# Decay attention: scores computed once and copied by ScalarE, the exponentials and the decay sharing one pair of PSUM banks

## The chip, the cores and the metric

One core of one Trainium2 chip runs a small language-model tower as one program. The metric is the device time in microseconds (us) of one execution; lower is better. A NeuronCore has TensorE (PE, matrix products, writes PSUM), VectorE (DVE), ScalarE (ACT, activation functions), GpSimd (POOL, which here works on SBUF alone) and DMA queues. Each engine takes its instructions in the order written, and engines wait for each other on semaphores.

## The reference, cut to what matters

The change lies in the attention of the second layer. For 128 sequences of 128 tokens, with 8 heads of width 8 and a causal mask, it computes

```python
scores = einsum('bhqd,bhkd->bhqk', q, k) / sqrt(dk)
p_ = softmax(where(mask, scores, -1e32)) * mask
distcum = cumsum(p_, axis=-1)
dist = sqrt(clip((p_.sum(-1) - distcum) * pos, 0))
total_effect = clip(exp(dist * gamma), 1e-5, 1e5)     # the decay
p = softmax(where(mask, scores * total_effect, -1e32))
out = einsum('bhqk,bhkd->bhqd', p, v)
```

So the scores are used twice: for a first softmax, whose running sum gives a decay for each pair of positions, and then, weighed by that decay, for the second softmax.

## The kernel before, in words

The phase is `phase_decay_attention`. Its work is cut into 128 steps K, each of two heads of four sequences; four steps (j = K mod 4 = 0 to 3) share the projections of one group of four sequences, m = K // 4. A tile of a step is 128 partitions by 768 numbers, 384 for each of the two heads (e), with the half that the mask hides largely left out (a long part of 512 and a short one of 256 over both heads). Keys are stored in reverse, so that a running sum gives what lies ahead.

The way of one step through the engines is:

- TensorE computes the scores into the bank pair `bS` (`scores`, lines 1486 and 1492).
- VectorE takes maxima (L1822, L1823) and subtracts them into `ex` (L1827, L1830), which counts `shifted`.
- ScalarE takes the exponential of `ex` in place (L1674).
- VectorE scans `ex` with the factors `cont` into `later` (L1861) and takes reciprocals of the totals.
- GpSimd multiplies by the distances (L1412, into `decay`) and by the reciprocals (L1416, L1417).
- ScalarE turns `decay` into its root and then the decay, with Ln, Exp and Exp (L1680, L1682, L1684).
- TensorE computes the same scores a second time, into the bank pair `bR`; VectorE multiplies them by the decay (L1838, into `p2`) and takes maxima (L1843, L1844); GpSimd subtracts these (L1429, L1430).
- TensorE transposes `p2` three tiles at a time into `bT` ("turn", L1505); ScalarE takes the exponential into `pT` (L1644), once for each of the two heads; TensorE weighs the values with it (L1523), and every second step turns the result back (L1621), which VectorE then normalises (L1875, L1880).

The steps are pipelined by hand: every engine has a loop over K in which the work of several steps is interleaved, and the order in that loop is the order of the queue. In iteration K, TensorE does the values (odd K), the turn of step K-3, head 0, then for j = 0 the convolution (L1563), then the scores of step K+1, the turn of step K-3, head 1, then the query or key projection (L1547), the transposes of the normalised input (j = 3), the turning back, and at the end the second scores, of step K-1. ScalarE does `pT` of step K-3, head 0, the exponential of step K, `pT` of step K-3, head 1, then the Ln, Exp, Exp of step K-1, and then copies of the group out of PSUM. VectorE does the maxima and subtraction of step K, the weighing of step K-2, and the scan of step K. GpSimd also issues the gather DMAs of a later group (L1423), adds, centres and scales the inputs of later groups, and makes `hTr`, the reversed copy of `hT` (L1442, L1443).

Before the scores of step K+1 may overwrite `bS`, TensorE waits in this kernel for

```python
pe.wait_ge(U["shifted"], 2 * (K + 1))
```

that is, for VectorE's subtraction of step K.

Of the kernel before, what the change touches and what calls it, by code (L numbers as in the profile page):

```python
# [6 lines left out]
ALU = mybir.AluOpType  # L7
# [6 lines left out]
P = 128  # L14
# [1278 lines left out]
def phase_decay_attention(nc, dram, H, slot, back_rows, ident, NB):  # L1293
# [10 lines left out]
    KEEP_V, KEEP_P, KEEP_T, KEEP_M = 3, 3, 8, 2  # L1304
    KEEP_Q, KEEP_D = 3, 3
    with ExitStack() as ctx:
# [32 lines left out]
        later = [m_.sb(f"d_later{u}", [P, 1 + 2 * SEG]) for u in range(2)]  # L1339
        p2 = [m_.sb(f"d_p2{u}", [P, 2, SEG]) for u in range(KEEP_P)]  # L1340
        pT = [m_.sb(f"d_pT{u}", [P, SEG]) for u in range(KEEP_T)]
        attT, inv = m_.sb("d_attT", [P, W]), m_.sb("d_inv", [P, GB, QUAD])
        y, yT = [m_.sb(f"d_y{u}", [P, GB, D]) for u in range(2)], m_.sb("d_yT", [P, 2 * P])

        bS, bR = [m_.ps(f"d_{name}", [P, 2, 512]) for name in ("S", "R")]
        bT, bO, X0, X1 = [m_.ps(f"d_{name}", [P, 512]) for name in ("T", "O", "X0", "X1")]
# [5 lines left out]
        U = {name: m_.sem(f"d_{name}") for name in  # L1352
             ("scored", "rescored", "max_made", "shifted", "exped", "scanned", "inv_total", "placed", "scaled", "log_done",
              "root_done", "decay_made", "weighed", "max2_made", "shifted2", "turned", "pT_kept")}
# [12 lines left out]
        def there(n):  # L1367
            return 0 <= n < NG
# [24 lines left out]
        with nc.Block() as block:  # L1393
# [9 lines left out]
            def _(pool):  # L1403
                pool.wait_ge(ready, READY)
                for K in range(FIRST, LAST + 1):
# [31 lines left out]
                    if j == 0:  # L1437
                        n = m + 1
                        if there(n):
                            pool.wait_ge(G["hT_kept"], n + 1)  # L1440
                            after(pool, "v_made", n - 1)
                            pool.tensor_copy(grouped(hTr[:, 0:2 * P], P), grouped(hT[:], P)[:, :, ::-1])  # L1442
                            pool.tensor_copy(grouped(hTr[:, 2 * P:SEG], HALF), grouped(hT[:], P)[:, :, HALF - 1::-1])\  # L1443
                                .then_inc(G["hTr_kept"], 1)
                        n = m + 3
                        if there(n):
                            pool.wait_ge(G["summed"], n + 1)
                            after(pool, "squared", n - 1)
                            pool.tensor_scalar(mean[:], mean[:], 1.0 / D, None, ALU.mult).then_inc(G["mean_made"], 1)
                            pool.wait_ge(G["mean_made"], n + 1)  # L1450
                            pool.tensor_tensor(hc[:], H[:, n * GB:(n + 1) * GB, :], over(mean[:], D), ALU.subtract)\
                                .then_inc(G["centred"], 1)
# [20 lines left out]
            def _(pe):  # L1473
# [76 lines left out]
                for K in range(FIRST, LAST + 1):  # L1550
# [35 lines left out]
                    if step_there(K + 1):  # L1586
                        if (K + 1) % PAIRS == 0:
                            pe.wait_ge(G["q_kept"], 2 * ((K + 1) // PAIRS + 1))
                            pe.wait_ge(G["k_kept"], (K + 1) // PAIRS + 1)
                        if K >= 0:  # L1590
                            pe.wait_ge(U["shifted"], 2 * (K + 1))
                        scores(K + 1, bS).then_inc(U["scored"], 1)
                    if step_there(K - 3):
                        turn(K - 3, 1)
                    if j == 0 and there(m + 1):
                        pe.wait_ge(G["hT_kept"], m + 2)
                        after(pe, "v_kept", m)
                        project(X0, 0, hT[:]).then_inc(G["q_made"], 1)
# [14 lines left out]
                    if K % 2 and quad_there(i):  # L1613
# [8 lines left out]
                        last.then_inc(Q["back"], 1)  # L1622
                    if step_there(K - 1):
                        if K >= 2:
                            pe.wait_ge(U["weighed"], K - 1)
                        scores(K - 1, bR).then_inc(U["rescored"], 1)

            @block.scalar
            def _(act):
# [21 lines left out]
                for K in range(FIRST, LAST + 1):  # L1651
                    m, j = K // PAIRS, K % PAIRS
                    i = (K - 5) // 2
                    if K % 2 and quad_there(i):
                        act.wait_ge(Q["attended"], i + 1)
                        if i >= 1:
                            act.wait_ge(Q["back"], i)
                        nc.scalar.activation(attT[:], bO[:], ACT.Copy).then_inc(Q["attT_kept"], 1)
# [13 lines left out]
                    if step_there(K):  # L1672
                        act.wait_ge(U["shifted"], 2 * (K + 1))
                        nc.scalar.activation(ex[K % 2][:], ex[K % 2][:], ACT.Exp).then_inc(U["exped"], 1)  # L1674
                    if step_there(K - 3):
                        keep_turned(K - 3, 1)
                    if step_there(K - 1):
                        u = (K - 1) % KEEP_D
                        act.wait_ge(U["scaled"], K)
                        nc.scalar.activation(decay[u][:], decay[u][:], ACT.Ln, bias=1e-18).then_inc(U["log_done"], 1)  # L1680
                        act.wait_ge(U["log_done"], K)
                        nc.scalar.activation(decay[u][:], decay[u][:], ACT.Exp, scale=0.5).then_inc(U["root_done"], 1)  # L1682
                        act.wait_ge(U["root_done"], K)
                        nc.scalar.activation(decay[u][:], decay[u][:], ACT.Exp, scale=-1.0).then_inc(U["decay_made"], 1)  # L1684
                    if j == 0:
                        n = m + 1
                        if there(n):
                            act.wait_ge(G["q_made"], n + 1)
                            if n >= KEEP_Q:
                                act.wait_ge(U["rescored"], PAIRS * (n - KEEP_Q + 1))  # L1690
                            for side in range(2):
                                out = grouped(qT[n % KEEP_Q][:].rearrange("p c x -> p (c x)"), P)
                                nc.scalar.activation(out[:, :, side * HALF:(side + 1) * HALF], grouped(X0[:], HALF),
                                                     ACT.Copy, scale=half[:, side:side + 1]).then_inc(G["q_kept"], 1)
                    if j == 1:
                        n = m + 1
                        if there(n):
                            act.wait_ge(G["k_made"], n + 1)
                            if n >= KEEP_Q:
                                act.wait_ge(U["rescored"], PAIRS * (n - KEEP_Q + 1))  # L1700
                            nc.scalar.activation(kT[n % KEEP_Q][:].rearrange("p c x -> p (c x)"), X1[:], ACT.Copy)\
                                .then_inc(G["k_kept"], 1)
# [23 lines left out]
                    if j == 3:  # L1726
# [9 lines left out]
                        if there(n):  # L1736
                            act.wait_ge(G["h_turned"], n + 1)
                            after(act, "q_made", n - 1)
                            after(act, "hTr_kept", n - 1)
                            nc.scalar.activation(hT[:], X0[:, 2 * P:4 * P], ACT.Copy).then_inc(G["hT_kept"], 1)  # L1740

            @block.vector
            def _(dve):
# [71 lines left out]
                for K in range(FIRST, LAST + 1):  # L1815
                    m, j = K // PAIRS, K % PAIRS
                    if step_there(K):
# [6 lines left out]
                        dve.wait_ge(U["max_made"], 2 * K + 1)  # L1824
                        if K >= 2:
                            dve.wait_ge(U["scanned"], K - 1)
                        nc.vector.tensor_tensor(long(ex[u]), long(bS), wide(mx[u], 1, P), ALU.subtract)\  # L1827
# [4 lines left out]
                    if step_there(K - 2):  # L1832
                        u, w, d = K % 2, (K - 2) % KEEP_P, (K - 2) % KEEP_D
                        dve.wait_ge(U["rescored"], K - 1)
                        dve.wait_ge(U["decay_made"], K - 1)
                        if K - 2 >= KEEP_P:
                            dve.wait_ge(U["turned"], 2 * (K - 1 - KEEP_P))
                        nc.vector.scalar_tensor_tensor(p2[w][:], decay[d][:], 1e-5, bR[:, :, 0:SEG],  # L1838
                                                       ALU.max, ALU.mult).then_inc(U["weighed"], 1)
                        dve.wait_ge(U["weighed"], K - 1)  # L1840
                        if K - 2 >= 2:
                            dve.wait_ge(U["shifted2"], K - 3)
                        nc.vector.tensor_reduce(mx2[u][:, 1], long(p2[w]), AX, ALU.max).then_inc(U["max2_made"], 1)  # L1843
                        nc.vector.tensor_reduce(mx2[u][:, 0], short(p2[w]), AX, ALU.max).then_inc(U["max2_made"], 1)  # L1844
# [503 lines left out]
```

## Time and profile before

| | |
|---|---|
| three runs | 2688.99, 2692.22, 2718.27 us; median 2692.22 |
| profiled execution | 2690.18 us, its span 2688.4 us |
| busy: PE / PEld / DVE / ACT / POOL | 79% / 60% / 64% / 48% / 63% of the span |
| the phase of the change | scans of its 128 steps start from 1393.4 to 2469.9 us |
| in that phase's 34.14 us group: POOL / PE / DVE / ACT | 32.70 / 31.77 / 27.72 / 21.73 us busy |
| granted clock of TensorE | 0.81 over the span, 0.80 in the group |

The busy shares over the whole span mix several phases; the phase of the change makes up some 40% of it, and is read by itself. There the work repeats with a period of 34.14 us, which is one group of four steps. The granted clock is 1.00 at 2.4 GHz and 0.50 at 1.2 GHz. A duration in a timeline row counts from the first instruction's start to the last one's end; consecutive instructions of an engine overlap a little, so the time that an instruction takes of its queue is read from start to start.

### The profile page before, as it was taken

How to read it: one execution, taken by the hardware profiler on the slowest of the kernel's cores; microseconds unless marked ns; L12 is line 12 of the kernel's file. 1: busy time of each engine (PE TensorE's matmuls, PEld its weight loads, DVE VectorE, ACT ScalarE, POOL GpSimd, SP SyncE). 2: the span in 40 equal slices, each digit the busy share in tenths (PEclk: the TensorE clock that was granted, in tenths of full speed). 3: DMA queues.
4: the chain of work that ended last, by engine and by line, in shares of the span. 5: the costliest groups of instructions: out<-in, count | busy, mean ns of one | idle time of the engine just before them, and what ended most of it. 6: DMA issues, size and time to landing. Idle time of an engine off the chain costs nothing. (4 is left out here: it accounts for less than half of the span.)

```text
span 2688.4 us, 55362 instructions
## 1 busy us (share of the span) xinstructions
PE 2128.1 (79%) x20380; PEld 1609.8 (60%) x20380; DVE 1707.4 (64%) x3444; ACT 1279.8 (48%) x2674; POOL 1695.7 (63%) x1921
## 2 busy tenths in 40 slices
PE   6999679999910029999459999999999988899485
PEld 5888557777710015555247777777777776676374
DVE  4899357777663004444438878888888888886424
ACT  1344146666610004444226666666666656665342
POOL 6564034444315764444179999999999999886271
PEclk9999569999955559999767877777777778975588
DMA  2111040000001125555200000000000000000003
GB/s 46 37 42 29 4 185 2 2 2 2 2 2 37 53 82 148 146 145 147 69 14 5 5 5 6 6 5 6 5 6 5 6 5 5 2 2 1 4 1 63
DMA packets 97288, 90.07 MB, mean 34 GB/s; under 512 B 55373, under 2 KB 82893, under 8 KB 97040
## 3 DMA queue, kind: packets, MB, share of 16 engines
q0 software_dynamic: 21616, 49.41, 6.4%
q1 hardware_dynamic: 75424, 37.32, 5.3%
q8 instruction: 159, 2.61, 0.4%
q14 instruction: 89, 0.73, 0.1%
HBM read 55.90 MB, written 30.79 MB: 32 GB/s over the span
## 5 line engine op out<-in xcount | busy, mean ns | idle before, releaser
L1861 DVE TENSOR_TENSOR_SCAN d_later<-d_cont,d_ex 128x768 f32<-128x768 f32 x128 | 280.7, 2193 | 25.3 <-ACT d_ex L1674 24.8
L1644 ACT ACTIVATE d_pT<-d_T 128x384 f32<-128x384 f32 x256 | 125.3, 489 | 297.2 <-PE d_T L1505 297.2
L1282 DVE TENSOR_TENSOR e_cont<-e_h,e_upto 128x512 f32<-128x512 f32 x91 | 62.9, 691 | 285.3 <-ACT e_upto L1181 285.3
L1412 POOL TENSOR_TENSOR d_decay<-d_later,d_posg 128x768 f32<-128x768 f32 x128 | 232.9, 1819 | 13.1 <-DVE d_later L1861 13.1
L1505 PE MATMUL d_T<-ident,d_p 128*128 128x128 f32 x768 | 172.3, 344 | 74.0 <-POOL d_p L1430 67.5
L1105 PE MATMUL e_X<-ident,e_xt 128*128 128x128 f32 x182 | 40.6, 305 | 198.0 <-DMA e_xt<-sent_rows 198.0
L1068 POOL DMA_INDIRECT sent_rows<-moe_rows,slot x128 | 124.9, 976 | 101.2 <-DVE slot L1258 62.5
L1429 POOL TENSOR_TENSOR d_p<-d_p,d_mx 128x512 f32<-128x512 f32 x128 | 167.3, 1307 | 30.1 <-DVE d_mx L1844 28.2
L1416 POOL TENSOR_TENSOR d_decay<-d_decay,d_rtot 128x512 f32<-128x512 f32 x128 | 170.9, 1335 | 19.0 <-POOL d_decay L1412 0.9
L1492 PEld LDWEIGHTS d_R<-d_kT,d_qT 16*128 16x128 f32 x2048 | 150.7, 221 | 51.0 <-issue 51.0
L1492 PEld LDWEIGHTS d_S<-d_kT,d_qT 16*128 16x128 f32 x2048 | 149.7, 220 | 51.8 <-issue 51.8
L1838 DVE SCALAR_TENSOR_TENSOR d_p<-d_decay,d_R 128x768 f32<-128x768 f32 x128 | 121.4, 948 | 85.0 <-PE d_R L1492 55.4
L1492 PE MATMUL d_R<-d_kT,d_qT 16*128 16x128 f32 (+1 forms) x2048 | 169.9, 313 | 0.0
L1492 PE MATMUL d_S<-d_kT,d_qT 16*128 16x128 f32 (+1 forms) x2048 | 168.8, 312 | 0.0
L1423 POOL DMA_INDIRECT d_moe<-back_rows,slot x128 | 128.7, 1006 | 62.4 <-DVE d_mean L1812 39.1
L1505 PEld LDWEIGHTS d_T<-ident,d_p 128*128 128x128 f32 x768 | 96.9, 166 | 101.2 <-POOL d_p L1430 76.6
L1105 PEld LDWEIGHTS e_X<-ident,e_xt 128*128 128x128 f32 x182 | 18.6, 143 | 228.5 <-issue 228.5
L1170 ACT ACTIVATE e_xT<-e_X,e_ln 128x256 f32<-128x256 f32 x91 | 43.2, 475 | 226.6 <-PE e_X L1105 226.6
L1087 POOL TENSOR_TENSOR e_ys<-e_yw 128x128 f32<-128x128 f32 x91 | 41.4, 455 | 168.3 <-DVE e_yw L1272 168.3
L1119 PE MATMUL e_h<-e_xT,e_wt 64*128 64x256 f32 x1092 | 145.2, 399 | 1.3 <-ACT e_xT L1170 1.3
L224 POOL DMA_INDIRECT rows<-in_table,idx x128 | 122.0, 953 | 35.6 <-issue 31.3
L1417 POOL TENSOR_TENSOR d_decay<-d_decay,d_rtot 128x256 f32<-128x256 f32 x128 | 141.9, 1108 | 0.0
(375 smaller groups left out, 6164.3 us busy)
## 6 DMA issues: line engine op xcount, KB each, us to landing
sent_rows<-b_blank SPq DMA_DIRECT2D x14, 845.0 KB, 11.1
e_xt<-sent_rows SPq DMA_DIRECT2D x91, 130.0 KB, 2.6
back_rows<-e_ys SPq DMA_DIRECT2D x91, 64.0 KB, 1.6
out_h<-g_Y SPq DMA_DIRECT2D x8, 512.0 KB, 4.0
rows<-in_table,idx POOLq DMA_INDIRECT x128
sent_rows<-moe_rows,slot POOLq DMA_INDIRECT x128, 2.3
d_moe<-back_rows,slot POOLq DMA_INDIRECT x128, 2.5
e_wt<-in_pair_w,e_pair POOLq DMA_INDIRECT x91
```

Of the source, the lines that this page charges most:

```text
L224: pool.indirect_dma_start(rows[u][:, b, :], None, dram["table"], bass.IndirectOffsetOnAxis(ap=idx[u][:, b:b + 1], axis=0))\
L1068: pool.indirect_dma_start(sent, bass.IndirectOffsetOnAxis(ap=slot[:, b:b + 1], axis=0), rows[:, b, :], None).then_inc(scattered[b // QUART ...
L1119: last = nc.tensor.matmul(bank[:, c // 2, c % 2 * TILE:(c % 2 + 1) * TILE], w[r, c * P:(c + 1) * P], xT[i % 2][r, :], start=True, stop=True)
L1412: pool.tensor_tensor(decay[d][:], later[u][:, 0:2 * SEG].rearrange("p (e s) -> p e s", e=2), posg[:, h:h + 2, :], ALU.mult).then_inc(U["pl ...
L1416: pool.tensor_tensor(long(decay[d]), long(decay[d]), wide(rtot[u], 1, P), ALU.mult)
L1417: pool.tensor_tensor(short(decay[d]), short(decay[d]), wide(rtot[u], 0, HALF), ALU.mult)\
L1423: pool.indirect_dma_start(moe[n % KEEP_M][:, j, :], None, back_rows, bass.IndirectOffsetOnAxis(ap=slot[:, b:b + 1], axis=0))\
L1429: pool.tensor_tensor(long(p2[w]), long(p2[w]), wide(mx2[u], 1, P), ALU.subtract)
L1492: last = nc.tensor.matmul(bank[:, e, cols], qT[s][r, c, (2 * g + S) * P:(2 * g + S + 1) * P], kT[s][r, c, keys], start=False, stop=(g == 1 ...
L1505: last = nc.tensor.transpose(bT[:, t * P:(t + 1) * P], p2[K % KEEP_P][:, e, t * P:(t + 1) * P], ident[:])
L1644: nc.scalar.activation(pT[w % KEEP_T][:], bT[:, 0:SEG], ACT.Exp).then_inc(U["pT_kept"], 1)
L1861: nc.vector.tensor_tensor_scan(later[u][:, 1:1 + 2 * SEG], cont[:], ex[u][:].rearrange("p e s -> p (e s)"), 0.0, ALU.mult, ALU.add)\
```

## The change

The scores are computed once. ScalarE copies them from `bS` into a new SBUF tile `sc` (three of them), and VectorE weighs that copy. The bank pair that held the second scores becomes `bE`, of which the first 768 columns, `inner`, hold in turn the exponentials of step K, read by the scan, and the decay of step K-2, read by the weighing. Both are written there by ScalarE. The decay's last exponential, of step K-2, moves from the end of iteration K-1 to the start of iteration K. `hTr` is now written by ScalarE out of PSUM, no longer by GpSimd. TensorE waits for `copied` where it waited for `shifted`. Below, the pieces stand in the order GpSimd, TensorE, ScalarE, VectorE; left out are the semaphores' names, waits on `rescored` that become waits on `scored`, and waits that go with the old buffers.

```diff
-        bS, bR = [m_.ps(f"d_{name}", [P, 2, 512]) for name in ("S", "R")]
+        sc = [m_.sb(f"d_sc{u}", [P, 2, SEG]) for u in range(KEEP_S)]
+        bS, bE = m_.ps("d_S", [P, 2, 512]), m_.ps("d_E", [P, 1024])
+        inner = bE[:, 0:2 * SEG]
...
-                            pool.tensor_copy(grouped(hTr[:, 0:2 * P], P), grouped(hT[:], P)[:, :, ::-1])
-                            pool.tensor_copy(grouped(hTr[:, 2 * P:SEG], HALF), grouped(hT[:], P)[:, :, HALF - 1::-1])\
-                                .then_inc(G["hTr_kept"], 1)
...
                         if K >= 0:
-                            pe.wait_ge(U["shifted"], 2 * (K + 1))
+                            pe.wait_ge(U["copied"], K + 1)
                         scores(K + 1, bS).then_inc(U["scored"], 1)
...
-                    if step_there(K - 1):
-                        if K >= 2:
-                            pe.wait_ge(U["weighed"], K - 1)
-                        scores(K - 1, bR).then_inc(U["rescored"], 1)
...
+                    if step_there(K - 2):
+                        act.wait_ge(U["root_done"], K - 1)
+                        act.wait_ge(U["scanned"], min(K, NQ))
+                        if K > NQ:
+                            act.wait_ge(U["weighed"], K - 2)
+                        nc.scalar.activation(inner, decay[(K - 2) % KEEP_D][:].rearrange("p e s -> p (e s)"), ACT.Exp,
+                                             scale=-1.0).then_inc(U["decay_made"], 1)
...
                     if step_there(K):
                         act.wait_ge(U["shifted"], 2 * (K + 1))
-                        nc.scalar.activation(ex[K % 2][:], ex[K % 2][:], ACT.Exp).then_inc(U["exped"], 1)
+                        nc.scalar.activation(sc[K % KEEP_S][:], bS[:, :, 0:SEG], ACT.Copy).then_inc(U["copied"], 1)
+                        if K >= 2:
+                            act.wait_ge(U["weighed"], K - 1)
+                        nc.scalar.activation(inner, ex[K % 2][:].rearrange("p e s -> p (e s)"), ACT.Exp).then_inc(U["exped"], 1)
...
-                        act.wait_ge(U["root_done"], K)
-                        nc.scalar.activation(decay[u][:], decay[u][:], ACT.Exp, scale=-1.0).then_inc(U["decay_made"], 1)
...
                             nc.scalar.activation(hT[:], X0[:, 2 * P:4 * P], ACT.Copy).then_inc(G["hT_kept"], 1)
+                            after(act, "v_made", n - 1)
+                            nc.scalar.activation(grouped(hTr[:, 0:2 * P], P), grouped(X0[:, 2 * P:4 * P], P)[:, :, ::-1], ACT.Copy)
+                            nc.scalar.activation(grouped(hTr[:, 2 * P:SEG], HALF), grouped(X0[:, 2 * P:4 * P], P)[:, :, HALF - 1::-1],
+                                                 ACT.Copy).then_inc(G["hTr_kept"], 1)
...
-                        nc.vector.scalar_tensor_tensor(p2[w][:], decay[d][:], 1e-5, bR[:, :, 0:SEG],
+                        nc.vector.scalar_tensor_tensor(p2[w][:], inner.rearrange("p (e s) -> p e s", e=2), 1e-5, sc[(K - 2) % KEEP_S][:],
                                                        ALU.max, ALU.mult).then_inc(U["weighed"], 1)
...
                         nc.vector.tensor_tensor_scan(later[u][:, 1:1 + 2 * SEG], cont[:],
-                                                     ex[u][:].rearrange("p e s -> p (e s)"), 0.0, ALU.mult, ALU.add)\
+                                                     inner, 0.0, ALU.mult, ALU.add)\
```

On TensorE, the stretch around iteration j = 1 read before (d_S and d_R are the two scores, d_T the turns and, from d_attT, the turning back, d_X the projections):

```order
L1492 MATMUL d_S<-d_kT,d_qT 128x128 x4
L1492 MATMUL d_S<-d_kT,d_qT 128x64 x4
L1505 MATMUL d_T<-ident,d_p 128x128 x3
L1546 MATMUL d_X<-d_ones,d_bqk_s 128x256
L1547 MATMUL d_X<-d_hTr,d_wqk 128x256
L1546 MATMUL d_X<-d_ones,d_bqk_s 128x256
L1547 MATMUL d_X<-d_hTr,d_wqk 128x256
L1621 MATMUL d_T<-ident,d_attT 128x128 x4
L1486 MATMUL d_R<-d_hide,d_ident_b 128x384 x2
L1492 MATMUL d_R<-d_kT,d_qT 128x128 x4
L1492 MATMUL d_R<-d_kT,d_qT 128x64 x4
L1505 MATMUL d_T<-ident,d_p 128x128 x3
```

and reads now:

```order
L1487 MATMUL d_S<-d_kT,d_qT 128x128 x4
L1487 MATMUL d_S<-d_kT,d_qT 128x64 x4
L1500 MATMUL d_T<-ident,d_p 128x128 x3
L1541 MATMUL d_X<-d_ones,d_bqk_s 128x256
L1542 MATMUL d_X<-d_hTr,d_wqk 128x256
L1541 MATMUL d_X<-d_ones,d_bqk_s 128x256
L1542 MATMUL d_X<-d_hTr,d_wqk 128x256
L1617 MATMUL d_T<-ident,d_attT 128x128 x4
L1500 MATMUL d_T<-ident,d_p 128x128 x3
L1566 MATMUL d_X<-d_wv,d_hTr 128x128 x2
```

The block of second scores is gone, and nothing takes its place: the turning back is followed by the turn of the next iteration.

On ScalarE, iteration j = 2 and the start of j = 3 read before (d_ex is the exponential for the scan, d_decay the three steps to the decay):

```order
L1674 ACTIVATE d_ex<-d_ex 128x768
L1644 ACTIVATE d_pT<-d_T 128x384
L1680 ACTIVATE d_decay<-d_decay 128x768
L1682 ACTIVATE d_decay<-d_decay 128x768
L1684 ACTIVATE d_decay<-d_decay 128x768
L1719 ACTIVATE d_v<-d_X 128x48x8
L1725 ACTIVATE d_yT<-d_X 128x256
L1658 ACTIVATE d_attT<-d_O 128x512
L1644 ACTIVATE d_pT<-d_T 128x384
L1674 ACTIVATE d_ex<-d_ex 128x768
```

and reads now (d_E is `inner`):

```order
L1673 ACTIVATE d_sc<-d_S 128x768
L1676 ACTIVATE d_E<-d_ex 128x768
L1636 ACTIVATE d_pT<-d_T 128x384
L1682 ACTIVATE d_decay<-d_decay 128x768
L1684 ACTIVATE d_decay<-d_decay 128x768
L1719 ACTIVATE d_v<-d_X 128x48x8
L1725 ACTIVATE d_yT<-d_X 128x256
L1651 ACTIVATE d_E<-d_decay 128x768
L1657 ACTIVATE d_attT<-d_O 128x512
L1636 ACTIVATE d_pT<-d_T 128x384
L1673 ACTIVATE d_sc<-d_S 128x768
```

The copy d_sc stands ahead of the exponential of the step; the decay's last exponential stands after the group's copies, at the start of the next iteration. The copy is one more instruction of 768 numbers for each step, behind both of the group's copies and of the decay.

## Rows read from the trace of the kernel before

**Rows 1.** Windows, one group of four steps and pieces of it: busy us (instructions), clock

```profile
core 0: us, PE busy (x) PEld busy (x) DVE busy (x) ACT busy (x) POOL busy (x), PEclk, DMA share, GB/s
1834.75:1868.89 34.14, 31.77 (x354) 25.16 (x354) 27.72 (x50) 21.73 (x39) 32.70 (x34) 0.80 0.03 5
1835.30:1854.30 19.00, 18.99 (x284) 14.19 (x282) 15.47 (x30) 12.48 (x24) 18.04 (x19) 0.99 0.02 6
1854.30:1856.05 1.75, 0.00 (x0) 0.00 (x0) 1.26 (x4) 1.69 (x3) 1.73 (x3) 1.00 0.15 19
1856.65:1866.70 10.05, 10.04 (x57) 8.22 (x58) 8.19 (x15) 5.74 (x11) 9.73 (x10) 0.50 0.02 3
1869.80:1873.00 3.20, 3.20 (x31) 2.34 (x29) 2.35 (x7) 0.58 (x2) 3.03 (x3) 1.00 0.05 10
```

**Rows 2.** Timeline of GpSimd: start, duration, engine, line, operation

```profile
1834.75 2.06 POOL L1417 TENSOR_TENSOR d_decay<-d_decay,d_rtot 128x256 f32<-128x256 f32 x1
...
1839.51 0.39 POOL L1442 COPY d_hTr<-d_hT 128x256 f32<-128x256 f32 x1
...
1839.86 0.28 POOL L1443 COPY d_hTr<-d_hT 128x128 f32<-128x128 f32 x1
...
1844.09 0.61 POOL L1417 TENSOR_TENSOR d_decay<-d_decay,d_rtot 128x256 f32<-128x256 f32 x1
...
1845.91 1.69 POOL L1429 TENSOR_TENSOR d_p<-d_p,d_mx 128x512 f32<-128x512 f32 x1
...
1854.99 1.05 POOL L1429 TENSOR_TENSOR d_p<-d_p,d_mx 128x512 f32<-128x512 f32 x1
...
1860.33 2.31 POOL L1416 TENSOR_TENSOR d_decay<-d_decay,d_rtot 128x512 f32<-128x512 f32 x1
```

**Rows 3.** The scan's line: count, duration ns min/median/max, first and last start

```profile
L1861 DVE TENSOR_TENSOR_SCAN d_later<-d_cont,d_ex x128: 1748/2026/3539, 1393.4 to 2469.9; 128x768 f32<-128x768 f32 x128
```

**Rows 4.** Timeline of VectorE: the longest of the four scans of the group

```profile
1858.86 2.95 DVE L1861 TENSOR_TENSOR_SCAN d_later<-d_cont,d_ex 128x768 f32<-128x768 f32 x1 [0.30 <-ACT d_ex L1674]
```

**Rows 5.** Timeline of TensorE: scores and turn at 2.4 GHz, then at 1.2 GHz

```profile
1836.24 0.49 PE L1486 MATMUL d_S<-d_hide,d_ident_b 128*128 128x384 bf16 x2
...
1837.70 0.55 PE L1505 MATMUL d_T<-ident,d_p 128*128 128x128 f32 x3
...
1858.21 0.85 PE L1486 MATMUL d_S<-d_hide,d_ident_b 128*128 128x384 bf16 x2
...
1860.89 0.90 PE L1505 MATMUL d_T<-ident,d_p 128*128 128x128 f32 x3
...
1866.73 2.98 PE L1563 MATMUL d_X<-d_conv,d_xT 128*128 128x128 f32 x13
```

**Rows 6.** Timeline of ScalarE in the same group

```profile
1838.29 0.49 ACT L1644 ACTIVATE d_pT<-d_T 128x384 f32<-128x384 f32 x1 [4.24 <-PE d_T L1505]
...
1844.94 0.49 ACT L1644 ACTIVATE d_pT<-d_T 128x384 f32<-128x384 f32 x1
...
1849.60 0.84 ACT L1674 ACTIVATE d_ex<-d_ex 128x768 f32<-128x768 f32 x1
...
1861.83 0.49 ACT L1644 ACTIVATE d_pT<-d_T 128x384 f32<-128x384 f32 x1 [3.01 <-PE d_T L1505]
```

**Rows 7.** Timeline of TensorE at 1.2 GHz: convolution; turn, then turning back

```profile
1420.71 4.47 PE L1563 MATMUL d_X<-d_conv,d_xT 128*128 128x128 f32 x20
...
2418.63 0.90 PE L1505 MATMUL d_T<-ident,d_p 128*128 128x128 f32 x3
...
2422.27 1.06 PE L1621 MATMUL d_T<-ident,d_attT 128*128 128x128 f32 x4
```

**Rows 8.** Timeline of VectorE: normalising, then the scores' maxima and subtractions

```profile
1863.55 0.26 DVE L1875 RECIPROCAL d_inv<-d_T 128x16 f32<-128x16 f32 x1 [1.46 <-PE d_T L1621]
...
1864.76 0.68 DVE L1822 TENSOR_REDUCE d_mx<-d_S 128x4 f32<-128x512 f32 x1
...
1866.62 0.94 DVE L1838 SCALAR_TENSOR_TENSOR d_p<-d_decay,d_R 128x768 f32<-128x768 f32 x1
```

More of the change, by code:

```diff
@@ L1304, in phase_decay_attention @@
     KEEP_V, KEEP_P, KEEP_T, KEEP_M = 3, 3, 8, 2
-    KEEP_Q, KEEP_D = 3, 3
+    KEEP_Q, KEEP_D, KEEP_S = 3, 3, 3
     with ExitStack() as ctx:
@@ L1352, in phase_decay_attention @@
         U = {name: m_.sem(f"d_{name}") for name in
-             ("scored", "rescored", "max_made", "shifted", "exped", "scanned", "inv_total", "placed", "scaled", "log_done",
+             ("scored", "copied", "max_made", "shifted", "exped", "scanned", "inv_total", "placed", "scaled", "log_done",
               "root_done", "decay_made", "weighed", "max2_made", "shifted2", "turned", "pT_kept")}
@@ L1437, in _ @@
                     if j == 0:
[L1438 to L1441, printed above, removed]
-                            pool.tensor_copy(grouped(hTr[:, 0:2 * P], P), grouped(hT[:], P)[:, :, ::-1])
-                            pool.tensor_copy(grouped(hTr[:, 2 * P:SEG], HALF), grouped(hT[:], P)[:, :, HALF - 1::-1])\
-                                .then_inc(G["hTr_kept"], 1)
                         n = m + 3
@@ L1596, in _ @@
                         pe.wait_ge(G["hT_kept"], m + 2)
+                        pe.wait_ge(G["hTr_kept"], m + 2)
                         after(pe, "v_kept", m)
@@ L1689, in _ @@
                             if n >= KEEP_Q:
-                                act.wait_ge(U["rescored"], PAIRS * (n - KEEP_Q + 1))
+                                act.wait_ge(U["scored"], PAIRS * (n - KEEP_Q + 1))
                             for side in range(2):
@@ L1699, in _ @@
                             if n >= KEEP_Q:
-                                act.wait_ge(U["rescored"], PAIRS * (n - KEEP_Q + 1))
+                                act.wait_ge(U["scored"], PAIRS * (n - KEEP_Q + 1))
                             nc.scalar.activation(kT[n % KEEP_Q][:].rearrange("p c x -> p (c x)"), X1[:], ACT.Copy)\
@@ L1738, in _ @@
                             after(act, "q_made", n - 1)
-                            after(act, "hTr_kept", n - 1)
                             nc.scalar.activation(hT[:], X0[:, 2 * P:4 * P], ACT.Copy).then_inc(G["hT_kept"], 1)
+                            after(act, "v_made", n - 1)
+                            nc.scalar.activation(grouped(hTr[:, 0:2 * P], P), grouped(X0[:, 2 * P:4 * P], P)[:, :, ::-1], ACT.Copy)
+                            nc.scalar.activation(grouped(hTr[:, 2 * P:SEG], HALF), grouped(X0[:, 2 * P:4 * P], P)[:, :, HALF - 1::-1],
+                                                 ACT.Copy).then_inc(G["hTr_kept"], 1)
             @block.vector
@@ L1824, in _ @@
                         dve.wait_ge(U["max_made"], 2 * K + 1)
-                        if K >= 2:
-                            dve.wait_ge(U["scanned"], K - 1)
                         nc.vector.tensor_tensor(long(ex[u]), long(bS), wide(mx[u], 1, P), ALU.subtract)\
@@ L1832, in _ @@
                     if step_there(K - 2):
-                        u, w, d = K % 2, (K - 2) % KEEP_P, (K - 2) % KEEP_D
-                        dve.wait_ge(U["rescored"], K - 1)
+                        u, w = K % 2, (K - 2) % KEEP_P
+                        dve.wait_ge(U["copied"], K - 1)
                         dve.wait_ge(U["decay_made"], K - 1)
```

## The prediction

> **What bounds the kernel now.** I read the clock and the windows first, then the timelines of the phase, engine by engine, over one period. The phase repeats every 34.14 us, four steps [rows 1]. GpSimd has no idle time in it: its queue goes from one instruction to the next, and the 1.4 us between the 32.70 us counted as busy and 34.14 lie around the issue of its gather DMAs. TensorE is busy for 31.77 us of it, VectorE for 27.72, ScalarE for 21.73 [rows 1]. So GpSimd sets the period, and TensorE is close behind.
>
> Part of GpSimd's time is blocked time. The reciprocals' product of 128x256 takes 0.61 us alone and 2.06 us where a scan runs beside it, which happens twice in a group (the second at 1851.8); the subtraction of 128x512 takes 1.05 us alone and 1.69; the product of the same size 2.31 [rows 2]. All four lie over a scan. Against the free durations that is 2 x 1.45 + 0.64 + 1.26 = 4.8 us per group. The scans pay too: 1748 ns is the shortest, 2026 the median, and one of each group takes 2.95 us [rows 3, 4].
>
> TensorE's clock matters as much. It is at the 2.4 GHz level from 1835.3 to 1856. TensorE stood idle from 1854.3, and the clock fell to 1.2 GHz; it stayed there for over 10 us in which TensorE worked without a pause on scores, turns and transposes [rows 1]. The convolution began at 1866.73, and by 1869.8 the clock was back at 2.4 GHz [rows 5, 1]. The group's mean of 0.80 means that some 40% of it is at 1.2 GHz.
>
> **The change part by part.**
>
> *GpSimd* loses the two copies for `hTr`, 0.39 + 0.28 = 0.67 us per group [rows 2]. The scan loses one of its two SBUF operands. If that ends the blocking, GpSimd needs 34.14 - 4.8 - 0.7 = 28.6 us per group. The trace shows only that the stretched instructions lie over the scan; it does not show why. The Trainium skill (SBUF — State Buffer, "Who interferes with whom") says that a VectorE instruction with two SBUF inputs contends with a GpSimd instruction that reads SBUF, and one with a single SBUF input does not. By that rule the blocking ends; without it GpSimd would keep 33.5 us. I take it as ended and price the other case as a rival.
>
> *TensorE* loses the second scores. They are the same instructions as the first, which take 1836.24 to 1837.70, 1.46 us, at 2.4 GHz and 1858.21 to 1860.89, 2.68 us, at 1.2 GHz [rows 5]; three of a group's four lie at the high clock now, so 7.1 us go. TensorE was idle for 2.4 us per group; in an unchanged period it would be idle for 9.5.
>
> *VectorE* keeps its instructions: its weighing already reads one operand from PSUM. Without the blocking it needs about 26 us per group. A scan that reads PSUM is in no row; I bound it by the shortest and the longest that there are with two SBUF operands, 1.75 and 2.95 us [rows 3, 4], and take 1.75, since the weighing beside it reads PSUM in 0.94 [rows 8]. At the high end VectorE would need 31 us, which still decides nothing below.
>
> *ScalarE* gains a copy of 768 numbers per step. The nearest row is the exponential of the same size, 0.84 us [rows 6]; two reads of 384 from PSUM would be 0.98 (2 x 0.49). I take 0.84; 0.98 adds 0.6 us per group. It also gains the reversed copies, 0.5 us per group from the copy sizes (GpSimd took 0.67; twice that is my upper end, 0.8 more). Its last exponential only moves. Exponentials written to PSUM may be a little shorter or longer than 0.84; I take them as equal. Its busy time becomes 21.7 + 3.4 + 0.5 = 25.6 us, less than any other engine's. By busy time alone nothing needs more than 28.6.
>
> *The new wait* is what I think decides. Up to now the scores of step K+1 waited for VectorE's subtraction; ScalarE could fall behind without holding TensorE. Now they wait for ScalarE's copy of step K. Behind them on TensorE's queue stands the turn of step K-3, head 1, and ScalarE's next instruction but one after the copy, `pT`, waits for that turn. After it, in order, stand Ln, Exp, the group's copies, the moved exponential, `pT` for head 0, and only then the copy of step K+1. So there is a closed loop through two engines, once per step: copy, scores, turn, all of ScalarE's work but one exponential, next copy. Only the exponential for the scan runs beside TensorE's part.
>
> TensorE's part is 1.46 us of scores, and 0.59 us from the turn's start to `pT`'s (1837.70 to 1838.29) [rows 5, 6], with some 0.05 for the semaphore 2.1 us; at 1.2 GHz it is 2.68 + 0.94 (1860.89 to 1861.83) + 0.05 = 3.7 us. ScalarE's part per group is its present busy time, 21.73, with the copies put in for the four exponentials that drop out of the loop, and 0.5 for `hTr`: 22.2 us. The loop is therefore 22.2 + 4 x 2.1 = **30.6 us** per group at 2.4 GHz throughout, and 22.2 + 4 x 3.7 = 37.0 at 1.2 GHz.
>
> At 1.2 GHz two detours are longer than the straight way. In step j = 1 VectorE must normalise the turned-back output before its maxima: scores 2.68, turn and key projection 3.64 (2418.63 to 2422.27), turning back 1.06, normalising 0.55 (twice some 0.26), maxima and subtractions 1.86 (1864.76 to 1866.62), copy 0.84, some 10.7 us [rows 7, 8]. The straight way is 3.7 and 4.66 (ScalarE from 1844.94 to 1849.60) and 0.84, 9.2: 1.5 us more [rows 6]. At the group's end the convolution, 4.3 us at the low clock [rows 7], can start only when ScalarE has copied its input, about 6.1 us after the copy `sc`; the next scores then wait until 10.4 against 8.9, 1.5 us more, of which 0.5 comes back since the clock rises during it. A group at 1.2 GHz throughout is 37.0 + 1.5 + 1.5 = **40.0 us**.
>
> **The clock decides between the two.** 34.14 = 30.6 + share x 9.4 gives a share of 0.38 at 1.2 GHz as the point of no change; today's is 0.40. And the loop makes TensorE wait in every step: at the high clock it has done the scores, the turns, the query projection and the values of step 0 some 5 us after the copy, and the next copy ends at 8.4. In the group shown, the fall came behind a single pause that began at 1854.3 [rows 1]. So I expect the clock to fall in the first or second step behind the convolution, and to rise only with the next convolution. Step 0 high, the other three low: 30.6 + 3 x 1.6 + 1.5 + 1.0 = 37.9 us per group, 3.8 more than now. From 1393.4 to 2469.9 there are 31.5 groups, of which I count 31: +117 us. Against the profiled execution's 2690.2 us (span 2688.4) that is 2807; the median of the runs, 2692.2, is the same within a tenth of a percent. This case alone spans 2750 to 2865, with the bounds for ScalarE's copies at the top and an earlier return of the clock at the bottom.
>
> **The rivals.**
> - *The clock stays up*, chance 0.13. The convolution and the projections come round every 8 us, and today's clock rides through shorter pauses. Then the group takes 30.6 us: -3.5 x 31 = -110, 2580 us. It decides from a share of 0.38 at 1.2 GHz downwards. Against it: more idle time than today in every step.
> - *The clock falls only after two steps*, 0.14: 30.6 + 2 x 1.6 + 1.0 = 34.8 us, +20, 2710 us.
> - *The clock never comes back*, 0.14, because TensorE's pauses also cut into the stretch with the convolution: 40.0 us, +182, 2872 us.
> - *Blocking stays*, and the loop is shorter than I make it, 0.08: only 0.67 us per group go, 33.5 us, 2669 us.
> - The forecast has the remaining 0.51.
>
> A measurement of this kernel tells about 1% (27 us) from no change. Faster by more: the first rival and a part of the fourth, 0.17. Within 1%: the rest of the fourth and most of the second, 0.13. Slower: 0.70. The range of 2665 to 2890 leaves out the first rival and the far end of the third, with the dearer bounds.
>
> **What will show it.** ScalarE's wait for the turns at `pT` should be in every step, and VectorE and GpSimd should now have idle time. GpSimd's 128x256 product at 0.6 us and scans at 1.75 us throughout would confirm the end of blocking. TensorE's first scores should start each time just after a `sc` copy ends. The granted clock in the phase should be near 0.6. I am wrong if the scores start later than the copy, held by something else, or if the clock stays at 0.8 or above.

## The result, and the profile after

| | before | changed kernel |
|---|---|---|
| median of 4 runs each | 2692.96 us | 2810.44 us |
| lowest and highest | 2688.99, 2718.27 | 2789.76, 2827.22 |
| ratio to before, 95% interval | | 1.0396 [1.0308, 1.0485] |
| profiled execution, its span | 2690.18, 2688.4 us | 2789.76, 2788.0 us |
| first and last scan's start | 1393.4, 2469.9 | 1387.5, 2573.0 |

The kernel is slower by 4.0%; the forecast was 2807 us. Here and below, ratios and intervals leave out the executions that lie over 1.5% above the fastest of the same kernel, so a ratio need not be the quotient of two medians. The profiled execution is the quickest of the four. Its span is 99.6 us longer than the one of before. Between first and last scan it takes 1185.5 us instead of 1076.5, 109 us more; the rest gives back 9. So all of it is in the phase of the change.

In the middle of that phase the period is now 37.55 us. The windows of one group, with the columns as in [rows 1], and stretches of it at one clock each:

```profile
core 0: us, PE busy (x) PEld busy (x) DVE busy (x) ACT busy (x) POOL busy (x), PEclk, DMA share, GB/s
1944.36:1981.91 37.55, 30.40 (x282) 22.62 (x282) 25.77 (x50) 24.42 (x45) 27.32 (x30) 0.68 0.02 5
1945.10:1951.40 6.30, 5.41 (x95) 3.44 (x93) 3.70 (x9) 4.27 (x7) 5.83 (x8) 1.00 0.02 4
1951.70:1964.90 13.20, 10.73 (x46) 6.89 (x46) 8.19 (x17) 8.33 (x17) 6.84 (x8) 0.50 0.03 5
1965.60:1971.80 6.20, 3.68 (x88) 2.67 (x84) 4.72 (x9) 5.01 (x10) 6.06 (x8) 1.00 0.01 4
1972.10:1981.80 9.70, 8.87 (x49) 7.97 (x47) 7.00 (x15) 6.20 (x12) 7.01 (x8) 0.51 0.03 8
```

Against [rows 1] GpSimd is busy 5.4 us less in a group that is 3.4 us longer, and no engine is busy without pause any more. The granted clock fell from 0.80 to 0.68, and it goes up and down twice in a group instead of once.

The blocking is gone. The scan's line (count, duration ns min/median/max, first and last start) answers to [rows 3], and the page's group of GpSimd's 128x512 subtraction (count, then busy us and mean ns) to the two durations of 1.69 and 1.05 us in [rows 2]:

```profile
L1862 DVE TENSOR_TENSOR_SCAN d_later<-d_cont,d_E x128: 1743/1750/1756, 1387.5 to 2573.0; 128x768 f32<-128x768 f32 x128
```

```profile
L1431 POOL TENSOR_TENSOR d_p<-d_p,d_mx 128x512 f32<-128x512 f32 x128 | 133.3, 1042 | 298.4 <-DVE d_mx L1845 298.0
```

All 128 scans take 1743 to 1756 ns; the longest was 3539 before. The subtraction takes its free time on average, and GpSimd now waits 298 us for VectorE's maxima ahead of it.

What ScalarE waits for shows in its timeline (start, duration, operation, idle time before it and who ended it). These are the copies and the `pT` of head 1, the ones behind the copies, which answer to [rows 6]:

```profile
1942.57 0.81 ACT L1673 ACTIVATE d_sc<-d_S 128x768 f32<-128x768 f32 x1 [0.71 <-DVE d_ex L1831]
...
1947.09 0.49 ACT L1636 ACTIVATE d_pT<-d_T 128x384 f32<-128x384 f32 x1 [2.85 <-PE d_T L1500]
...
1952.43 0.82 ACT L1673 ACTIVATE d_sc<-d_S 128x768 f32<-128x768 f32 x1
...
1956.90 0.49 ACT L1636 ACTIVATE d_pT<-d_T 128x384 f32<-128x384 f32 x1 [2.94 <-PE d_T L1500]
...
1963.23 0.81 ACT L1673 ACTIVATE d_sc<-d_S 128x768 f32<-128x768 f32 x1 [0.34 <-DVE d_ex L1831]
...
1966.76 0.49 ACT L1636 ACTIVATE d_pT<-d_T 128x384 f32<-128x384 f32 x1 [1.84 <-PE d_T L1500]
...
1970.97 0.83 ACT L1673 ACTIVATE d_sc<-d_S 128x768 f32<-128x768 f32 x1
...
1975.21 0.49 ACT L1636 ACTIVATE d_pT<-d_T 128x384 f32<-128x384 f32 x1 [2.71 <-PE d_T L1500]
...
1980.12 0.81 ACT L1673 ACTIVATE d_sc<-d_S 128x768 f32<-128x768 f32 x1 [0.71 <-DVE d_ex L1831]
```

ScalarE stands idle ahead of each of these `pT`, 10.3 us in the group. The page's groups of `pT`, before and now (count, busy us and mean ns, idle time before it, and who ended it), give it over the whole phase:

```profile
L1644 ACT ACTIVATE d_pT<-d_T 128x384 f32<-128x384 f32 x256 | 125.3, 489 | 297.2 <-PE d_T L1505 297.2
```

```profile
L1636 ACT ACTIVATE d_pT<-d_T 128x384 f32<-128x384 f32 x256 | 126.7, 495 | 352.6 <-PE d_T L1500 352.4
```

So ScalarE waited for turns before too, 297 us against 352 now. What is new is that TensorE in its turn waits for ScalarE's copy. These are the rows of TensorE at the group's second step:

```profile
1945.05 0.49 PE L1481 MATMUL d_S<-d_hide,d_ident_b 128*128 128x384 bf16 x2
...
1949.97 0.55 PE L1500 MATMUL d_T<-ident,d_p 128*128 128x128 f32 x3
1953.31 0.82 PE L1481 MATMUL d_S<-d_hide,d_ident_b 128*128 128x384 bf16 x2 [2.80 <-ACT d_sc L1673]
1954.06 1.97 PE L1487 MATMUL d_S<-d_kT,d_qT 16*128 16x128 f32 x16
1955.96 0.90 PE L1500 MATMUL d_T<-ident,d_p 128*128 128x128 f32 x3
```

The scores behind this copy start at 1953.31, 0.06 us after the copy's end (1952.43 + 0.82), TensorE having waited 2.80 us for it. In the next two steps they start 0.06 and 0.15 us after the copy's end; only behind the copy at 1942.57 does the convolution lie between, and they start 1.67 us after it, at 1945.05. The turn begins at 1955.96, `pT` at 1956.90. That is the link, once at 1.2 GHz.

### The profile page after: what moved, and what is told of

Read it like the earlier page. It is cut to its first block and busy times, and to the rows that moved or that the text cites. A ratio compares the mean times of both kernels' runs of the same rounds, so it can differ in the third digit from the quotient of the medians.

```text
span 2788.0 us, 50854 instructions
## 1 busy us (share of the span) xinstructions
PE 2084.4 (75%) x18076; PEld 1535.9 (55%) x18076; DVE 1646.6 (59%) x3444; ACT 1367.4 (49%) x2866; POOL 1528.8 (55%) x1857
## 5 line engine op out<-in xcount | busy, mean ns | idle before, releaser
L1636 ACT ACTIVATE d_pT<-d_T 128x384 f32<-128x384 f32 x256 | 126.7, 495 | 352.6 <-PE d_T L1500 352.4
L1431 POOL TENSOR_TENSOR d_p<-d_p,d_mx 128x512 f32<-128x512 f32 x128 | 133.3, 1042 | 298.4 <-DVE d_mx L1845 298.0
L1862 DVE TENSOR_TENSOR_SCAN d_later<-d_cont,d_E 128x768 f32<-128x768 f32 x128 | 224.0, 1750 | 17.3 <-ACT d_E L1676 17.3
L1500 PE MATMUL d_T<-ident,d_p 128*128 128x128 f32 x768 | 191.1, 375 | 55.1 <-DVE d_y L1881 52.5
L1487 PEld LDWEIGHTS d_S<-d_kT,d_qT 16*128 16x128 f32 x2048 | 187.7, 270 | 61.9 <-issue 61.9
L1487 PE MATMUL d_S<-d_kT,d_qT 16*128 16x128 f32 (+1 forms) x2048 | 208.8, 364 | 0.0
L1839 DVE SCALAR_TENSOR_TENSOR d_p<-d_E,d_sc 128x768 f32<-128x768 f32 x128 | 121.8, 951 | 137.6 <-issue 132.4
L1481 PE MATMUL d_S<-d_hide,d_ident_b 128*128 128x384 bf16 x256 | 85.6, 428 | 141.8 <-ACT d_sc L1673 140.8
L1418 POOL TENSOR_TENSOR d_decay<-d_decay,d_rtot 128x512 f32<-128x512 f32 x128 | 133.0, 1039 | 19.0 <-POOL d_decay L1414 0.9
L1558 PE MATMUL d_X<-d_conv,d_xT 128*128 128x128 f32 x640 | 139.5, 414 | 1.5 <-ACT d_xT L1733 1.5
L1558 PEld LDWEIGHTS d_X<-d_conv,d_xT 128*128 128x128 f32 x640 | 138.8, 330 | 3.0 <-ACT d_xT L1733 3.0
```

Of the source, the lines that this page charges most:

```text
L1418: pool.tensor_tensor(long(decay[d]), long(decay[d]), wide(rtot[u], 1, P), ALU.mult)
L1431: pool.tensor_tensor(long(p2[w]), long(p2[w]), wide(mx2[u], 1, P), ALU.subtract)
L1487: last = nc.tensor.matmul(bank[:, e, cols], qT[s][r, c, (2 * g + S) * P:(2 * g + S + 1) * P], kT[s][r, c, keys], start=False, stop=(g == 1 ...
L1500: last = nc.tensor.transpose(bT[:, t * P:(t + 1) * P], p2[K % KEEP_P][:, e, t * P:(t + 1) * P], ident[:])
L1558: last = nc.tensor.matmul(X1[:, g * P:(g + 1) * P], xT[:, g, tap:tap + P], conv[:, tap, :], start=(tap == 0), stop=(tap == TAPS - 1))
L1636: nc.scalar.activation(pT[w % KEEP_T][:], bT[:, 0:SEG], ACT.Exp).then_inc(U["pT_kept"], 1)
```

## The experiments

All ten are edits of the kernel before or of the changed kernel. "Group" is four times the distance from first to last scan over 127, so a mean over the phase of the profiled execution; by that count the kernel before has 33.91 us and the changed one 37.34. "Ratio" is to the kernel before, which ran beside each experiment (medians from 2689.72 to 2693.6 us). The changed kernel did not run again beside them; differences from it are taken from its median of 2810.44 us.

### The changed kernel with the loop opened by the turn's place

```diff
+                    if step_there(K - 3):
+                        turn(K - 3, 1)
                     if step_there(K + 1):
...
                             pe.wait_ge(U["copied"], K + 1)
                         scores(K + 1, bS).then_inc(U["scored"], 1)
-                    if step_there(K - 3):
-                        turn(K - 3, 1)
```

> The changed kernel with one edit: on TensorE the turn of step K-3, head 1, goes ahead of the scores of step K+1, and so ahead of their wait for ScalarE's copy. Loop theory: ScalarE no longer waits for TensorE between two copies; it has 25.6 us of work per group, GpSimd 28.6, VectorE 26; the group falls from 37.55 us to 29 to 33 us, the kernel to some 2530 to 2660 us, and ScalarE's idle time before pT mostly goes. Rival (the lower clock alone makes the group long, TensorE being at its limit at 1.2 GHz): the turn's place changes nothing, 37 to 38 us per group, 2790 to 2830 us. Rival (ScalarE's added copies are the cost): likewise unchanged.

Measured: 2629.22 us median, ratio 0.9758 [0.9689, 0.9827]; group 31.86 us. One block moved on one queue takes 181 us off the changed kernel and makes it faster than the one before. ScalarE's wait for the turns over the whole phase fell from 352.4 us to 69.1 (the page's group: count, busy us and mean ns, idle time before):

```profile
L1636 ACT ACTIVATE d_pT<-d_T 128x384 f32<-128x384 f32 x256 | 126.0, 492 | 69.2 <-PE d_T L1500 69.1
```

The loop theory holds; neither the low clock by itself (from 1450 to 2350 us the mean granted clock is 0.74, in the changed kernel 0.68) nor ScalarE's added work, which is all still there, explains the changed kernel's time.

### The kernel before with the new wait alone

```diff
-                            pe.wait_ge(U["shifted"], 2 * (K + 1))
+                            pe.wait_ge(U["exped"], K + 1)
```

> The kernel before with one edit: the scores of step K+1 wait for ScalarE's exponential of step K, not for VectorE's subtraction; no copy, no other bank, no moved exponential. Loop theory: the wait by itself closes the loop; 21.7 us of ScalarE and four links of 2.1 to 3.7 us give 30.1 us at the high clock and 36.5 us and two detours at the low one, where TensorE, still with its second scores, also nears 47 us; the group grows from 34.14 to 36 to 41 us, the kernel to 2750 to 2900 us. Rival (the wait is harmless, it is the scores' late copy or the idle TensorE that costs): 34.1 us, 2690 us.

Measured: 2872.97 us, ratio 1.0711 [1.0604, 1.0819]; group 39.72 us. The wait by itself is enough for a loss, a larger one than the whole change brings. ScalarE's idle time before `pT` is 544.8 us here, against 297.2 in the kernel before:

```profile
L1644 ACT ACTIVATE d_pT<-d_T 128x384 f32<-128x384 f32 x256 | 125.8, 491 | 545.0 <-PE d_T L1505 544.8
```

That the changed kernel loses less than this one fits what it takes away from TensorE, 7 us of second scores per group. The experiment does not part the loop from the clock, though: from 1450 to 2350 us the granted clock is 0.69, against 0.82 in the kernel before, and TensorE is busy for 835.8 of these 900 us. How much of the loss is the loop's length and how much is TensorE's own work at the lower clock is not shown.

### The changed kernel with the scan reading SBUF

```diff
-                        nc.scalar.activation(inner, ex[K % 2][:].rearrange("p e s -> p (e s)"), ACT.Exp).then_inc(U["exped"], 1)
+                        nc.scalar.activation(ex[K % 2][:], ex[K % 2][:], ACT.Exp).then_inc(U["exped"], 1)
...
-                                                     inner, 0.0, ALU.mult, ALU.add)\
+                                                     ex[u][:].rearrange("p e s -> p (e s)"), 0.0, ALU.mult, ALU.add)\
```

VectorE's wait for `scanned` ahead of the subtraction comes back with it.

> The changed kernel with the exponentials for the scan again in SBUF (ex, in place), so that the scan has two SBUF operands; all else stays. Operand theory: the stretched instructions on GpSimd come back, 128x256 products of some 2 us and scans over 1.75 us, 3 to 5 us per group, but GpSimd at 33 us per group is not the bound: 37.5 to 38.5 us per group, 2790 to 2830 us. Rival (the scan's operand has nothing to do with it, the other phase between the engines ended the overlap): GpSimd's durations stay at 0.6 and 1.04 us, time unchanged. Rival (the end of blocking is what keeps the changed kernel from being slower still): the group grows by 3 to 5 us, to 41 or 42, 2890 to 2940 us.

Measured: 2790.9 us, ratio 1.0392 [1.0323, 1.0461]; group 36.83 us. The long durations are back, in some of the scans and in GpSimd's subtractions (1042 to 1677 ns on average), though hardly in the 128x256 products (610 to 702 ns), where I had expected them; and the time does not move:

```profile
L1864 DVE TENSOR_TENSOR_SCAN d_later<-d_cont,d_ex x128: 1747/1758/3581, 1394.2 to 2563.6; 128x768 f32<-128x768 f32 x128
```

```profile
L1431 POOL TENSOR_TENSOR d_p<-d_p,d_mx 128x512 f32<-128x512 f32 x128 | 214.6, 1677 | 123.1 <-DVE d_mx L1847 121.6
```

So the scan's second SBUF operand is what blocks, as the Trainium skill (SBUF — State Buffer, "Who interferes with whom") has it. The other versions bear this out against the rival of a shifted phase: the six with the scan from PSUM have groups from 30.5 to 37.3 us and no scan over 1757 ns, and each of the six with two SBUF operands has a scan of 2621 ns or more. In the changed kernel it makes no difference to the time that the blocking is gone.

### The same with the loop open

Both edits: the turn ahead of the scores, and the scan from SBUF.

> The changed kernel with the turn ahead of the scores, and the scan's exponentials back in SBUF. Operand theory: with the loop open GpSimd is near the bound again, and its blocked time of 3 to 5 us per group lengthens the group from 31 to 33.4 us (the turn alone) to 33.5 to 35 us, 2665 to 2720 us; so this is where the gain of the second bank pair's new use sits. Rival (the end of blocking is worth nothing in any version): 2615 to 2640 us, as the turn alone.

Measured: 2721.29 us median, four runs from 2676.22 to 2728.32, too far apart for a ratio; the group of the profiled execution (2723.76 us) is 34.55 us against 31.86 with the scan from PSUM. The scan's line:

```profile
L1864 DVE TENSOR_TENSOR_SCAN d_later<-d_cont,d_ex x128: 1747/2190/3847, 1395.9 to 2492.8; 128x768 f32<-128x768 f32 x128
```

From 1450 to 2350 us GpSimd is busy for 821 us, 31.5 us per group, where the turn alone has 753, 26.6 per group. VectorE's wait that came back with the edit shows no idle time. Once the loop is open, the blocking therefore costs time: 2.7 us per group, some 85 us over the phase, in the profiled executions, and 62 us between the lowest runs of the two versions (2676.22 and 2614.56). The turn alone is some 60 us faster than the kernel before, so without the end of blocking little or nothing would be left of that gain.

### The changed kernel with TensorE kept at work

```diff
+                    if step_there(K) and K < NQ - 1 and K >= 5:
+                        pe.wait_ge(Q["attT_kept"], i + 1)
+                        for _ in range(2):
+                            nc.tensor.matmul(bO[:], ident[:], wqk[:], start=True, stop=True)
                     if step_there(K + 1):
```

The products' result is not read by anyone.

> The changed kernel with two idle-time products of 128x128x512 numbers per step on TensorE, into bank bO while nobody uses it, ahead of the scores' wait; their result is never read. They take some 1.7 us of TensorE per step at the high clock, twice that at the low one. Clock theory: they keep the clock at 2.4 GHz through the group, and the loop runs at its high-clock length of 30.6 to 32 us per group, 2580 to 2640 us, granted clock in the phase above 0.9. Rival (the clock is a symptom and not a part of the cost): the group stays at 37.5 us or grows with the added work, to 38 to 41 us, 2800 to 2910 us.

Measured: 2656.42 us, ratio 0.9868 [0.9808, 0.9928]; group 32.87 us, the mean granted clock from 1450 to 2350 us is 0.98. So 154 us of the changed kernel's time hang on the clock, with the loop closed as before; that is net of what the products themselves cost. The group is 0.9 us longer than my upper figure and the time 16 us. The profile gives a reason: the odd steps' products wait for `attT`, 1.1 and 0.5 us in the group looked at, and then stand in front of the scores. No run thus shows the closed loop at the high clock by itself, which I had put at 30.6 us. The step with the longer wait:

```profile
1894.54 0.55 PE L1500 MATMUL d_T<-ident,d_p 128*128 128x128 f32 x3
1896.19 1.98 PE L1584 MATMUL d_O<-d_wqk,ident 128*128 128x512 f32 x4 [1.10 <-ACT d_attT L1661]
1898.01 0.49 PE L1481 MATMUL d_S<-d_hide,d_ident_b 128*128 128x384 bf16 x2
```

### Both: loop open, clock high

> Both edits of the changed kernel: the turn ahead of the scores' wait, and two idle-time products of 128x128x512 per step into bO. Loop and clock theory together: the loop is open and the clock is high; what is left is GpSimd's 28.6 us of work per group and the way of one step through VectorE and ScalarE; 28.5 to 31 us per group, 2540 to 2610 us, below the turn alone (2629). Rival (with the loop open TensorE's clock no longer matters): the same as the turn alone, 2615 to 2640 us. Rival (the added products stand in the way of the scores at their wait for attT): slower than the turn alone, 2640 to 2680 us.

Measured: 2592.23 us, ratio 0.9592 [0.9504, 0.9681]; group 30.51 us, clock 0.99 from 1450 to 2350 us. The profiled execution, 2622.84 us, is the longest of the four; its first scan starts at 1435.8 us, where the turn alone has 1394.2, so that surplus lies ahead of the phase and not in the group. It is the fastest version, 218 us below the changed kernel. Its scans sit 30.65 us apart per group without variation through most of the phase. ScalarE waits 14.2 us for turns in the whole phase.

### The same, with the added work in even steps alone

Three products in even steps and none in odd ones (`and K % 2 == 0` in the condition).

> The changed kernel with the turn ahead of the scores and three idle-time products of 128x128x512 into bO in even steps alone, where they need not wait for ScalarE's attT. Theory (in the version with two per step the products' wait in odd steps costs some of the gain): 29 to 30.5 us per group, 2540 to 2590 us. Rival (the clock falls in the odd steps without them): 31 to 33 us per group, 2610 to 2640 us.

Measured: 2678.43 us (10 runs), ratio 0.9925 [0.9882, 0.9969]; group 33.46 us. My theory fell; the rival named the right effect, and the time lies above its range too: without the products the clock falls in an odd step, and the next even step's three products then start at 1.2 GHz ahead of the scores. They take 4.01 us there, and the granted clock is 0.50 until 1920.0, for the first 2.5 us of them:

```profile
1916.87 0.85 PE L1500 MATMUL d_T<-ident,d_p 128*128 128x128 f32 x3
1917.51 4.01 PE L1586 MATMUL d_O<-d_wqk,ident 128*128 128x512 f32 x6
1921.36 0.49 PE L1481 MATMUL d_S<-d_hide,d_ident_b 128*128 128x384 bf16 x2
```

It is worse than the turn alone (2629): the added work paid in the version where it held the clock all the way, and not in this one.

### The copy made by VectorE

```diff
+                        nc.vector.tensor_copy(sc[K % KEEP_S][:], bS[:, :, 0:SEG]).then_inc(U["copied"], 1)
...
-                        nc.scalar.activation(sc[K % KEEP_S][:], bS[:, :, 0:SEG], ACT.Copy).then_inc(U["copied"], 1)
```

> The changed kernel with the copy of the scores made by VectorE, behind its subtraction, instead of by ScalarE; the turn stays behind the scores. The scores' wait is then for VectorE again, as in the kernel before. Loop theory: the loop through ScalarE is open by another way than in the turn's case; VectorE has 26 + 4 x 0.95 = 29.8 us of work per group; 31 to 34 us per group, 2600 to 2690 us. Rival (what helped was the turn's earlier place, not the open loop): 37 us per group, 2790 us or more, VectorE being loaded further.

Measured: 2630.88 us, ratio 0.9756 [0.9678, 0.9834]; group 31.89 us. The turn is where it was, and the time is that of the turn's experiment to within 2 us. By itself this run could also mean that ScalarE is better off without the copies; but the turn's experiment left them on ScalarE and gained as much. What the two have in common is that the loop through ScalarE is open, whichever edge of it is cut.

### Two controls on the kernel before

One idle-time product per step (as above, `range(1)`), and, apart from it, the turn ahead of the scores.

> The kernel before with one idle-time product of 128x128x512 per step into bO ahead of the scores' wait; nothing else. GpSimd theory for the kernel before: its queue has no idle time, so a higher clock of TensorE changes at most the places where blocking falls: 33 to 34.6 us per group, 2660 to 2710 us. Rival (the kernel before too is held by TensorE's low clock): a group of 30 to 32 us, 2570 to 2640 us. Rival (TensorE, 93% busy, has no room): slower, 2720 to 2800 us.

> The kernel before with the turn of step K-3, head 1, ahead of the scores of step K+1. Loop theory: in this kernel no loop goes through that turn, since the scores wait for VectorE, and GpSimd is the bound: 33.5 to 34.7 us per group, 2670 to 2715 us. Rival (an earlier turn helps by itself, whatever the scores wait for): 2600 to 2660 us, as much as it gave the changed kernel's successor.

Measured: with the product 2704.09 us (10 runs), ratio 0.9988 [0.9942, 1.0033], group 33.66 us, clock 0.94 from 1450 to 2350 us where the kernel before has 0.82. With the turn moved 2721.63 us (10 runs), ratio 1.011 [1.0074, 1.0147], group 34.50 us. The kernel before gains nothing from a higher clock nor from the earlier turn, the two edits that take 154 and 181 us off the changed one. GpSimd, busy for 851 to 852 of the 900 us in all three, is left as what held it; no run took work off GpSimd alone there. The second control is even 1% slower. Its trace shows most of that in GpSimd's own time: busy for 32.6 us per group instead of 32.1, with the issues of the gather DMAs (L1423) at 1252 ns on average instead of 1018. What makes them longer was not tested.

## Why the prediction was right

Most terms can be set against the group that begins with the copy at 1942.57. The prediction gives 8.4 + 1.0 and 10.7 us for the first two steps; the other two get equal parts of what is left of its sum. From copy to copy the four steps take:

| step | forecast | measured |
|---|---|---|
| j = 0, with the convolution's delay | 8.4 + 1.0 | 9.86 |
| j = 1, 1.2 GHz, by way of VectorE | 10.7 | 10.80 |
| j = 2, 1.2 GHz | 8.9 | 7.74 |
| j = 3, 1.2 GHz | 8.9 | 9.15 |
| sum | 37.9 | 37.55 |

- **The bound before**, GpSimd without idle time: right as far as the controls go, which rule out TensorE's clock and the turn's place.
- **The end of blocking**: right, scans of 1.75 us throughout, GpSimd busy 5.4 us less per group against 4.8 + 0.67 forecast, and of no worth while the loop is closed. The rival in which it stays is out.
- **ScalarE's added work**: the copy 0.81 for 0.84 us, the two reversed copies 0.39 and 0.29 where I counted 0.5 together; busy 24.4 us per group against the 25.6 forecast, where I added durations that overlap a little. That 25.6 would be "less than any other engine's" was a slip: TensorE's 31.77 less 7.1 is 24.7 at the old clock. Nothing in the sum rests on it.
- **The link**: at the high clock 1945.05 to 1947.09, 2.04 us for 2.05 (before the semaphore); at the low one 1953.25, the copy's end, to 1956.90, 3.65 for 3.7. The 0.05 us for the semaphore, for which the prediction had no row, is 0.06.
- **The detour through VectorE** in step 1: right. The copy at 1963.23 is released by VectorE's subtraction, as is the one at 1980.12 in step 3, which I had on the straight way.
- **The clock** fell where it was expected, in step 0's wait. That it would rise only with the next convolution was wrong: it was at 2.4 GHz again from 1965.6, behind the key and value projections, and fell once more by 1972. Step 2 was therefore shorter by 1.2 us, with the sum nearly right since steps 0 and 3 took 0.7 more. The forecast of the mean clock, near 0.6, should have been 0.68.

The likeliest case was right in its mechanism: the new wait closes a loop through ScalarE, as the turn's experiment and the copy on VectorE show, and the lower clock lengthens it, as the products show. Its size was right to 0.35 us per group. Times the 31 groups it gave +117 us; the phase grew by 109 and the whole profiled execution by 99.6. The medians also differ by 117 us, and that closeness is luck: misses of 1.2 and 0.7 us largely cancel within the group, and the four runs differ by 37 us among themselves.

What stays open: why the group of the best version stops at 30.5 us and not at GpSimd's 28.6. Its waits are spread over four engines, none above 60 us in 500, and no run took it apart.

## What to carry to other kernels

Before a wait is moved from one engine to another, follow the queue behind the waiting instruction: if the new releaser, further down its own queue, waits for something queued behind it, the two engines' times add up, however idle each looks. Then move what the releaser needs ahead of the wait. And a wait put on TensorE can come back as a lower clock: the new wait alone took it from 0.82 to 0.69 with all of TensorE's work kept. What work taken off TensorE is worth has to be priced at the clock that is left.

## What the runs showed that I had not expected

Being busy did not by itself bring the 2.4 GHz level back: in the kernel before, TensorE ran 10 us without pause on scores, turns and transposes at 1.2 GHz, and the clock rose only behind the start of the convolution [rows 1, 5]. In the changed kernel it rose at some 1965.4, behind the key and value projections, after a stretch in which TensorE was busy for 10.73 of 13.20 us. Which instructions bring the rise was not isolated.

A higher clock did not need a busier TensorE either. From 1450 to 2350 us the changed kernel with two products per step has a clock of 0.98 with TensorE busy for 784 of the 900 us, over 4 us idle per group; the kernel before has 0.82 with 825. The products' cost was less than their gain, by 154 us.
